# A two-layer transformer: the last feed-forward of layer 0 placed inside layer 1's first trip

## The reference, cut to what matters

```python
# layer 0, per block of sequences
x1 = x0 + attention(h) @ Wo.T
y  = causal_conv(x1, taps) + b
g  = silu(qy @ w_gate) * (qy @ w_up)       # qy: y rounded to 8 bits per row
x2 = x1 + quantise(rms_norm(g)) @ w_down
# layer 1, per block
n  = rms_norm(x2) * scale(cond) + shift(cond)
xc = small_attention(n @ W_qkv) @ W_out + n
xl = layer_norm(xc)
x3 = x2 + rotary_attention(xl) @ Wo1
y3 = causal_conv(x3, taps)
out = x3 + relu(y3 @ w_fc) ** 2 @ w_proj
```

## Time and profile before

| | |
|---|---|
| median of the runs | 1660.3 us (1657.55 to 1661.77, three runs) |
| the profiled execution | 1647.16 us, of which the span from first to last instruction 1645.4 us |
| PE busy | 1446.9 us, 88% of the span |
| DVE busy | 1121.2 us, 68% |
| ACT busy | 861.2 us, 52% |
| POOL busy | 396.4 us, 24% |
| layer 0's `last_chunk` ends on PE (last `gate_up` of block 6) | at 973.7 us |
| the code between the layers ends, `chunk1(0)` begins | at 1049.0 us |
| `chunk1(1)` begins | at 1115.0 us |

### The profile page before, as it was taken

How to read it: one execution, slowest core, us unless ns; L and a number is a source line. 1 busy time by engine, 2 the same in 40 slices (tenths; PEclk the granted TensorE clock), 3 DMA queues, 4 the chain that set the end, 5 groups by cost and what they waited for, 6 DMA issues and landing times.

```text
span 1645.4 us, 26036 instructions
## 1 busy us (share of the span) xinstructions
PE 1446.9 (88%) x8786; PEld 1115.0 (68%) x8786; DVE 1121.2 (68%) x2646; ACT 861.2 (52%) x1740; POOL 396.4 (24%) x320
## 2 busy tenths in 40 slices
PE   6999999887999999999899675878889898989897
PEld 6766766556777777778687552645667585766766
DVE  3988998943464646666665756747686868678685
ACT  4766766755566667575755635443443434343311
POOL 2766666621221212130221000100102020110102
PEclk9998998998999999999999876889899999999999
DMA  9122222233010101011011301000000000000000
GB/s 364 40 52 52 52 52 78 52 94 144 26 33 26 39 32 57 13 51 38 25 38 67 141 1 64 20 0 14 14 7 14 6 13 6 13 6 7 14 7 13
DMA packets 24867, 73.51 MB, mean 45 GB/s; under 512 B 3796, under 2 KB 4438, under 8 KB 23256
## 3 DMA queue, kind: packets, MB, share of 16 engines
q1 hardware_dynamic: 24504, 71.66, 13.7%
q10 hardware_dynamic: 288, 0.85, 0.2%
HBM read 49.43 MB, written 23.07 MB: 44 GB/s over the span
## 4 chain that ended last, share of the span: by engine, by line
PE 43%; issue 24%; DVE 21%; ACT 6%; POOL 5%; DMA 0%; DVEq 0%; POOLq 0%; SPq 0%; ACTq 0%
PE psum L932 8%; PE psum L903 7%; POOL stats L1690 5%; PE psum L523 3%; PE psum L942 3%; PE psum L539 3%; PE psum L588 3%; DVE work L1788 2%; PE psum L849 2%; ACT probs_t L1470 2%; PE psum L693 2%; PE psum L634 1%; PE psum L515 1%; DVE work L1857 1%; PE psum L621 1%
## 5 line engine op out<-in xcount | busy, mean ns | idle before, releaser
L588 PE MATMUL psum<-h_all,w_big 128*128 (+1 forms) x1024 | 245.2, 386 | 6.0 <-ACT ident_bf L1200 4.4
L588 PEld LDWEIGHTS psum<-h_all,w_big 128*128 128x128 f32 x1024 | 189.8, 193 | 41.4 <-issue 12.6
L1690 POOL TENSOR_TENSOR stats<-stats,minus_half 128x32 f32<-128x32 f32 x15 | 102.5, 6836 | 360.9 <-ACT stats L1233 360.9
L932 PE MATMUL psum<-w_big 128*128 128x256 f32 x512 | 132.5, 419 | 23.3 <-ACT w_big L1499 23.3
L1788 DVE SCALAR_TENSOR_TENSOR work<-work,taps 128x248 f32<-128x248 f32 (+30 forms) x558 | 151.4, 349 | 0.1
L932 PEld LDWEIGHTS psum<-w_big 128*128 128x128 f32 x512 | 106.6, 212 | 49.6 <-ACT w_big L1499 31.4
L539 PE MATMUL psum<-w_big,h_all 128*64 128x512 f32 x512 | 125.8, 635 | 5.4 <-ACT w_emb L1153 5.4
L523 PEld LDWEIGHTS psum<-gru_mem 128*128 128x128 f32 x768 | 96.3, 206 | 37.6 <-DVE gru_mem L1888 24.9
L1788 DVE SCALAR_TENSOR_TENSOR h_all<-h_all,taps 128x248 f32<-128x248 f32 (+30 forms) x434 | 116.1, 343 | 0.1
L523 PE MATMUL psum<-gru_mem 128*128 128x128 f32 x768 | 102.1, 294 | 15.7 <-DVE gru_mem L1888 15.7
L903 PE MATMUL psum<-work,w_big 128*128 128x256 f32 x512 | 115.3, 379 | 0.0
(11 more groups left out here) (267 smaller groups left out, 2909.4 us busy)
## 6 DMA issues: line engine op xcount, KB each, us to landing
value_rows<-w_emb SPq DMA_DIRECT2D x128, 128.0 KB, 2.3
work<-value_rows SPq DMA_DIRECT2D x16, 1024.0 KB, 5.7
w_big<-in_Wq SPq DMA_DIRECT2D x2, 2048.0 KB, 15.1
w_big<-in_Wo SPq DMA_DIRECT2D x2, 2048.0 KB, 20.6
out<-w_big SPq DMA_DIRECT2D x16, 256.0 KB, 2.1
x_res<-out SPq DMA_DIRECT2D x15, 256.0 KB, 2.8
work<-in_w SPq DMA_DIRECT2D x1, 2048.0 KB, 12.0
w_big<-in_Wv SPq DMA_DIRECT2D x1, 2048.0 KB, 16.1
```

What stands on the lines that cost most here:

```text
L588: mm = pe.matmul(bank(n % 2)[:, o * TA:(o + 1) * TA], w_big[:, s, k * H * HD + at:k * H * HD + at + HD], h_all[:, k, bass.ds(i * BA, BA), ...
L932: mm = pe.matmul(bank(2 + g)[:, 0:D], o1_t[:, h, g * P:(g + 1) * P], wo1[:, h, :], start=(h == 0), stop=(h == H - 1), skip_group_check=True)
L1690: pool.tensor_tensor(qk_r, qk_ms, minus_half[:, 0:2 * GA * HU], ALU.pow).then_inc(r_on.sem, 1)
```

## The change

The order of five programs is rewritten around the border of the layers; no operation is left out and none is computed in another way.

- The code between the layers is gone. The small attention of block 0 is moved up into `last_chunk(7)`: its rows are normalised ahead of `take_scores` 1 to 3, turned and scaled ahead of the last softmax, and its steps are placed between the feed-forward steps of block 6, whose end now also lies there.
- The convolution of block 7 is cut: lags 0 to 15 run on DVE in `last_chunk(7)`, lags 16 to 31 in `chunk1(0)`.
- The feed-forward of block 7 and `turn_w5` run inside `chunk1(0)` (`begun` is true there, `e` = 7).
- To make room, the feed-forward of block 7 gets a second set of hidden buffers in the last quarter of `w_big` (`hid_of`), the rotary outputs of block 0 go to `gru_mem` (`o1_first`), the w5 weights are read back in eight pieces into `h_all` and `w_emb`, and the small attention of block 0 uses other banks. The two-bank variant of the last feed-forward (`gu_bank`, `sil_of`) is dropped; it runs in banks 6 and 7 as the others do.
- `chunk1(0)` no longer waits for `x2_on` at its start; PE waits for it before `cond_outputs(1, 0)`, and for the last w5 piece before `chunk1(1)`.

```diff
-        w5_back = gru_mem[:, 0:NBLK * BLK]
+        w5_back = [h_all.rearrange("p k b t -> p (k b t)")[:, n * 512:(n + 1) * 512] for n in range(7)] + [w_emb[:, 512:1024]]
+        hid_of = [hidden_bufs(gru_mem[:, 4096:8192]), hidden_bufs(w_big[:, 3, :])]
+        o1_first = gru_mem[:, 0:4096].rearrange("p (h n) -> p h n", h=H)
```

On SP, in `last_chunk`:

```diff
+                sp.wait_ge(x1_on.sem, NA * GA)
+                sp.wait_ge(xn_on.sem, 1)
+                sp.dma_start(x_c, out[:, GA:2 * GA, :]).then_inc(xc_in, 16)
+                sp.wait_ge(w5_out, 16 * len(W5_PARTS))
+                for n in range(PIECES):
+                    sp.dma_start(w5_back[n], w5_dram[:, n * 512:(n + 1) * 512]).then_inc(w5_again, 16)
                 store_x2(i - 1)
```

On PE, in `last_chunk`, behind the last unit's scores:

```diff
+                pe.wait_ge(ms_on.sem, UNITS)
+                turn_rows(0)
                 turn_y(c)
+                pe.wait_ge(wa_in, 16 * 2)
+                pe.wait_ge(xnt_on.sem, 1)
+                pe.wait_ge(proj_kept.sem, UNITS * TILES)
+                cond_qk(0, 0)
+                cond_qk(0, 1)
                 turn_yq(c)
                 pe.wait_ge(yqt_on.sem, c + 1)
                 gate_up(c, 0)
                 outputs(v)
                 gate_up(c, 1)
                 pe.wait_ge(ot_on.sem, PAIRS * UNITS)
-                pe.wait_ge(proj_kept.sem, UNITS * TILES)
+                pe.wait_ge(cqkv_kept.sem, 2)
                 residual(i, (0,))
                 gate_up(c, 2)
+                cond_v()
+                pe.wait_ge(cqkv_kept.sem, 3)
+                cond_turn(0, 0)
                 residual(i, (1,))
                 gate_up(c, 3)
+                cond_scores(0, 0)
+                cond_turn(0, 1)
+                turn_x1(i)
+                down_turn(c, 0)
+                cond_scores(0, 1)
+                down(c, 0)
+                down_turn(c, 1)
+                pe.wait_ge(w_out_on.sem, 1)
+                cond_outputs(0, 0)
+                cond_project(0, 0)
+                down(c, 1)
+                turn_rows(1)
+                cond_outputs(0, 1)
+                cond_project(0, 1)
```

On PE, in `chunk1`. The first piece stands in the first trip in place of the stretch from `q_heads` 10 to the first eight heads of `rot_project`, the second behind `fc`:

```diff
+                if begun:
+                    turn_y(e)
+                    q_heads(i, range(10, 12))
+                    turn_yq(e)
+                    pe.wait_ge(yqt_on.sem, e + 1)
+                    gate_up(e, 0)
+                    q_heads(i, range(12, 14))
+                    gate_up(e, 1)
+                    cond_scores(ci, 0)
+                    cond_turn(ci, 1)
+                    q_heads(i, range(14, H))
+                    gate_up(e, 2)
+                    rot_scores(i, 0)
+                    rot_scores(i, 1)
+                    gate_up(e, 3)
+                    cond_scores(ci, 1)
+                    down_turn(e, 0)
+                    down(e, 0)
+                    rot_outputs(i, 0)
+                    down_turn(e, 1)
+                    rot_outputs(i, 1)
+                    rot_project(i, 0, range(0, 8))
+                    down(e, 1)
+                    pe.wait_ge(x2_on.sem, NA * GA)
...
+                if begun:
+                    pe.wait_ge(w5_again, 16 * PIECES)
+                    turn_w5(range(PIECES))
                 if prep:
                     turn_rows(i + 2)
```

On ACT, in `last_chunk`, `row_squares(0)` now stands behind `keep_hidden(c - 1, 1)` and `scale_rows(0)` behind `keep_means(v)`; then:

```diff
+                keep_cond_qk(0, 0, 1)
+                keep_cond_qk(0, 1, 2)
                 exps(v)
                 keep_yq(c)
                 spread_probs(v)
                 silu(c, 0)
                 keep_outputs(v, 1, range(PAIRS))
                 silu(c, 1)
                 hidden_squares(c, 0)
                 silu(c, 2)
+                act.wait_ge(pads_on.sem, 2)
+                keep_cond_v(0)
+                keep_cond_turned(0, 0)
                 silu(c, 3)
+                keep_cond_turned(0, 1)
+                keep_x1(i)
                 hidden_squares(c, 1)
+                keep_hidden(c, 0)
+                cond_exps(0, 0)
+                row_squares(1)
+                spread_cond_probs(0, 0)
+                cond_exps(0, 1)
+                keep_hidden(c, 1)
+                scale_rows(1)
+                keep_cond_outputs(0, 0)
+                spread_cond_probs(0, 1)
+                keep_cond_outputs(0, 1)
+                apply_norm(0)
```

On ACT, in `chunk1(0)`, `keep_y`, `keep_yq`, `silu` 0 and 1 and `hidden_squares(e, 0)` stand ahead of `keep_cond_turned(ci, 1)`, and `silu` 2 and 3 behind it; then:

```diff
                     rot_exps(i, 0)
                     rot_exps(i, 1)
+                if begun:
+                    hidden_squares(e, 1)
                 if cond:
                     cond_exps(ci, 0)
+                if begun:
+                    keep_hidden(e, 0)
                 if rot:
                     keep_rot_outputs(i, 0)
                 if cond:
                     spread_cond_probs(ci, 0)
+                if begun:
+                    keep_hidden(e, 1)
                 if rot:
                     keep_rot_outputs(i, 1)
```

On DVE, in `last_chunk`:

```diff
                 conv1(range(22, T))
+                film_rows(0, clink)
                 soft_in(v)
                 quantise_y(c, flink)
                 soft_out(v)
+                cond_rms(0, clink)
+                cond_norm(0, 0, clink)
+                cond_norm(0, 1, clink)
                 hidden(c, 0, (0, 1))
...
                 hidden(c, 1, (1,))
                 weigh(c, 1)
+                cond_soft_in(0, 0, clink)
                 quantise_hidden(c, 1, hlink)
+                conv_last(range(0, 4))
+                cond_soft_out(0, 0, clink)
+                cond_soft_in(0, 1, clink)
+                add_ffn(c, 0)
+                conv_last(range(4, 8))
+                cond_soft_out(0, 1, clink)
+                add_ffn(c, 1)
+                conv_last(range(8, 12))
+                layer_norm(0, clink)
+                film_rows(1, lambda ins: link(ins, c_step, 1))
+                conv_last(range(12, 16))
```

On DVE, in `chunk1`:

```diff
                     cond_norm(ci, 1, clink)
+                if begun:
+                    conv_last(range(16, T))
                 turn_heads(4)
+                if begun:
+                    quantise_y(e, lambda ins: link(ins, ffn_step, e))
+                    hidden(e, 0, (0,))
+                    turn_heads(2)
+                    hidden(e, 0, (1,))
+                    weigh(e, 0)
+                    turn_heads(2)
+                    hidden(e, 1, (0,))
+                    quantise_hidden(e, 0, elink)
                 turn_heads(H)
                 if rot:
                     rot_soft_in(i, 0, rlink)
                     rot_soft_in(i, 1, rlink)
+                if begun:
+                    hidden(e, 1, (1,))
+                    weigh(e, 1)
+                if rot:
                     rot_soft_out(i, 0, rlink)
                 if cond:
                     cond_soft_in(ci, 0, clink)
+                if begun:
+                    quantise_hidden(e, 1, elink)
+                    hid_step.end_trip()
                 if rot:
                     rot_soft_out(i, 1, rlink)
                 if cond:
                     cond_soft_out(ci, 0, clink)
+                if begun:
+                    add_ffn(e, 0)
+                    add_ffn(e, 1)
```

More of the change, by code:

```diff
@@ L330, in x1_bank, with hid_bufs, o1_of @@
             return bank(3) if isinstance(c, int) and c >= NA - 2 else bank(7)
[L332 to L346, removed]
+        def hid_bufs(c):
+            return hid_of[isinstance(c, int) and c == NA - 1]
+        def o1_of(c):
+            return o1_first if isinstance(c, int) and c == 0 else o1_t
         def rows_of(c):
@@ L1054, in chunk1 @@
                     pj(ni, range(GA))
-            c = NA - 1
-            turn_rows(0)
-            turn_x1(c)
-            down_turn(c - 1, 0)
-            down(c - 1, 0)
-            down_turn(c - 1, 1)
-            pe.wait_ge(wb_in, 16 * 4)
-            pe.wait_ge(xnt_on.sem, 1)
-            cond_qk(0)
-            down(c - 1, 1)
-            pe.wait_ge(cqkv_kept.sem, 1)
-            cond_qk(1)
-            cond_v()
-            pe.wait_ge(cqkv_kept.sem, 3)
-            cond_turn(0, 0)
-            cond_scores(0, 0)
-            cond_turn(0, 1)
-            turn_y(c)
-            cond_scores(0, 1)
-            pe.wait_ge(w_out_on.sem, 1)
-            cond_outputs(0, 0)
-            turn_yq(c)
-            cond_project(0, 0)
-            pe.wait_ge(yqt_on.sem, c + 1)
-            pe.wait_ge(x2_on.sem, GA * c)
-            gate_up(c, 0)
-            gate_up(c, 1)
-            cond_outputs(0, 1)
-            gate_up(c, 2)
-            cond_project(0, 1)
-            gate_up(c, 3)
-            down_turn(c, 0)
-            down(c, 0)
-            pe.wait_ge(w5_again, 16)
-            turn_w5(range(0, 4))
-            turn_rows(1)
-            down_turn(c, 1)
-            down(c, 1)
-            turn_w5(range(4, 8))
-            pe.wait_ge(x2_on.sem, NA * GA)
+            pe.wait_ge(wqk_in, 16 * 2)
+            pe.wait_ge(h_kept.sem, T + 1)
+            pe.wait_ge(const_on.sem, 8)
+            for n in range(QK_TILES):
+                qk_tiles(0, 0, (n,))
+                if n % 2 == 0 and n:
+                    square_sums(0, n // 2 - 1)
+            value_tiles(T // 2 - 1, 0)
+            square_sums(0, 3)
```

(29 more changed lines are left out.)

245 lines of the change are left out of this document (87 added, 158 removed).

## The result

The changed kernel takes 1663.45 us (median of 20 runs, 1658.42 to 1670.4), the kernel before 1659.38 us (20 runs, 1655.97 to 1665.38): the ratio is 1.003, 95% interval 1.0018 to 1.0042. That is 4.07 us more by the medians (5.0 by the ratio), where the forecast added 4.5 to the median it had. The interval lies on both sides of the bound of 0.3%, so the kernel is neither clearly slower nor clearly the same by it.

What follows compares the result with a forecast made beforehand. The prediction took the order of hand-offs around PE's in-order stream as the bound. Full-clock 1107.0 plus 12.5 of clock gave 1119.5 against 1115.0; 4.5 added to the 1660.3 median gave 1664.8 us, range 1655 to 1671.

Steps and rivals of the forecast that it cites:

- the bound of 0.3%: What the kernel's runs can tell apart, 5.0 us; the forecast difference stood just inside it.
- The schedule: New order from last softmax of layer 0 through first trip of layer 1, laid out with start-to-start durations, then clock loss.
- the sum: Start of the next trip: 1107.0 at full clock plus 12.5 of clock gives 1119.5, against 1115.0 before, 4.5 us later.
- The part beside the softmax: Small attention of block 0 moved beside layer 0's last softmax: first trip starts 41.0 us earlier, 1008.0 against 1049.0.
- the clock term: PE work behind each wait runs at half clock: 17 to 18 us, some 5 absorbed in waits, leaving 12.5.
- the edits counted at nothing: Second hidden buffers, `o1_first`, bank changes, eight-piece w5 load, block 2's rows, ACT tables and POOL order: no cost.
- Rival (c): First trip of layer 1: DVE hand-offs run closer, 2 to 3 us less, ending at +2, 1662.3; chance 0.10.
- +1.3 at full clock: To the next trip's start, clock loss left out on both sides: 1105.7 before, 1107.0 after, 1.3 later.
- Rival (a): Every group behind a wait at half clock, nothing absorbed: 17.5 instead of 12.5, +9.5, 1669.8; chance 0.15.
- Rival (b): PE's clock stays up: 3.5 earlier if 4.5 is lost, 8.0 earlier (1652.3) if nothing is; chance 0.10.
- Rival (d): Rows of block 2 or w5 wait behind other DMAs and hold `turn_rows`(2): about +6, 1666; chance 0.05.

Runs made afterwards that it cites:

- the old order filled: Kernel before the change, with PE products that compute nothing added in seven waits from 980 to 1040 us: 1654.46 us, ratio 0.9974.
- its filled run: Changed kernel with PE products that compute nothing added in five waits: 1655.52 us, ratio 0.9984 to the kernel before.
- `down` first: Changed kernel with PE doing `down`(7,1) ahead of the eight heads of `rot_project`: 1656.17 us, ratio 0.9974 to the kernel before.
- hidden copy first: Changed kernel with ACT doing the copy `keep_hidden`(7,0) ahead of `cond_exps`(1,0): 1660.28 us, ratio 0.9999 to the kernel before.
- the kernel with the block standing alone: Changed kernel with block 7's lags, feed-forward and w5 turns ahead of the first trip of layer 1, not inside: 1658.7 us, ratio 1.0009 to the kernel before.
- the four orders: Changed kernel with `keep_hidden`(7,0), heads 10 and 11, `down`(7,1) and `cond_soft_in`(1,1) each moved earlier: 1656.79 us, ratio 0.9983 to the kernel before.

## Why the prediction was right

**The schedule held.** With the offset of 13.74 taken off, the first trip starts at 1011.6 (said: 1007 to 1012) and the second at 1119.0 (said: 1117 to 1122, the sum 1119.5). The waits: 10.77 for 11.0, 6.52 for 7.3, 6.91 for 7.5, 3.42 for 3.4, 3.65 for 3.8, 3.50 for 4.4; the lags 16 to 31 took 6.51 for 6.4, DVE stood 10.25 at the add for 9. The part beside the softmax gave 37.4 us for the 41.0 at full clock, and the trip is 107.4 long for 99.0: 3.6 and 8.4 us more, together 12.0 where the clock term had 12.5. The w5 turns took 5.4 for 6.4, and none of the edits counted at nothing shows: no transfer is waited for, neither w5's nor that of the rows of block 2.

**The cover that the change counts on is not there in this order.** The first trip took in the work at its full price, 41.9 for 42.0 us. Rival (c), hand-offs closer than summed, has a little in it: of the waits just listed all but that before `turn_yq` came out 0.2 to 0.9 shorter than summed, yet the whole is at +4.0, nearer to the sum's 4.5 than to its +2. That it lies only 0.4 from the sum is in part luck: the prediction put its own error at about 3 us, and shorter waits and longer rows (the start of the trip lost 2.8 for the 1.7 summed) make up for each other.

**The clock.** The term was needed. The rows behind waits are long on both sides: after, 6.49 for 3.96 (outputs) and 5.54 for 3.72 (the projection); before, 6.11 and 5.65. An estimate from the timelines of all runs, each row less the shortest of its shape and count: between the first `outputs` and the second trip PE's rows lose some 22 us after and some 19 before. The difference of 3 is that of the sum; the 22 are more than the 17 to 18 that were listed. How much of it lies on the path is less sure than the 12.5 had it: filling waits gave back 5.2 and 4.2 to 4.9.

I had made the difference from +1.3 at full clock and +3.2 of clock (12.5 less 9.3). The measured 4.1 can be split by one more place. From the start of the first trip to the first turn of its small attention PE runs without a wait, in 16.86 us before (1065.86 - 1049.0) and 16.85 with the old order filled, but 19.70 after and 19.71 in its filled run, since the trip now begins behind a wait of 4.04. These 2.8 us are clock, and they reach `turn_y`: where the stretch was 0.8 shorter by chance (`down` first, hidden copy first), `turn_y` stood 0.8 nearer to the start of the trip (26.0 for 26.8). With both filled, 2.9 to 3.6 less 2.8 leaves 0.1 to 0.8 for the order at full clock, where I had 1.3. This split is worked out, not tested: no run filled the wait of 4.04. In the kernel with the block standing alone the trip starts at full clock (16.88) and D is 192.6 all the same; there the loss stands ahead of the trip.

The Trainium skill, "TensorE: Matmul & The Clock Gate", Part 1: The HAM clock gate, puts the penalty of the ramp below 1% of a typical kernel span and advises against fitting it. The prediction read this as said of all half-clock work behind waits, which is more than the sentence covers. The 5 us that filling gave back are 0.3% of the 1660 us of the kernel and 2.6% of D, and more than the difference of the two kernels.

**Rival (a)**, nothing absorbed, asked for +9.5 and is out at +4.0. **Rival (b)**, faster because the clock stays up, did not happen by itself: the clock did not stay up (0.87 and 0.80 in the two windows of the trip). Where it was kept up by filling, the old order gained nearly as much, so that the comparison stayed on the same side. **Rival (d)**, a late transfer, does not occur.

**What the text had not seen.** It called the 11.0 before `down`(7,0) the widest new gap and gave the 9 us of DVE at the add one sentence. The experiments put the worth the other way round: 4.4 us off the one gave 0.0, and one swap at the other gave 4.4.

## What to carry to other kernels

Idle time in a later stage does not by itself hide work that is moved there: here it cost 41.9 us for the 42.0 it takes alone, since its steps stood in queues behind the stage's own. What it costs depends on the order in those queues, and four swaps took 7 us off it. Do not rank gaps by their width: move the thing that ends the gap, see whether the next waits on the same engine grow by as much, and look for an engine that stands in its queue with the next stage's first operation behind it. When a change is worth a few us, compare a local distance between two rows of the same program part, not the spans.

## What the hardware showed

- Two profiled executions of the same kernel, the one before, have the first `outputs` 14 us apart (926.50 and 940.65) and spans of 1645.4 and 1659.7, with D equal to 0.2 us.
- PE work that computes nothing shortened both kernels: D is 5.2 us less with the new order, and 4.9 with the old, of which 4.2 behind the first filling (ratio 0.9974, 0.9959 to 0.9989). With the four orders it gave nothing.
- The same instructions up to `turn_y`(7) took 111.2 us from the first `outputs` in two executions (`down` first, hidden copy first) and 111.9 to 112.2 in three others; in the two, the clock rose one group of products earlier (the third group of the trip took 1.89 for 2.60).
- ACT's change of table (1.28 us at 1075.94) ran ahead of the wait for the data of the exponential, which started at 1079.00: it lay in ACT's idle time and cost nothing.
